# Bias matmul of the gates: contraction padded from 3 rows to 128

## The chip, the cores and the metric

The kernel runs on one core of a Trainium2 chip. The metric is the device time of one execution in microseconds (us), the median over several runs of the same program.

## The reference

There are 64 graphs of 128 nodes with 128 features. Each graph goes through an attention layer with a residual and a layer norm, and then through a relational layer with a residual and a layer norm. Cut to what the inputs leave (the adjacency holds only 0 and 1, so a single kind of edge and the `loop` relation matter), it is:

```python
# layer 0
e = leaky_relu(einsum('bid,bjd->bij', x * a_0[:, 0], x), 0.2)
alpha = softmax(where(adj == 1, e, NEG_INF))
y = layernorm(x + einsum('bij,bjd->bid', alpha, x))
# layer 1: one direction, one relation
h = y @ W_loop.T
g = h @ Wg_loop.T
vals = (h + b_loop) * sigmoid(g + bg_loop)
out = layernorm(y + relu(einsum('bnm,bmd->bnd', adj_t == 1, vals)))
```

The gates step makes `h + b_loop` and `g + bg_loop` for every node. The bias is one row of 256 numbers, the same for every node.

## The kernel before

The 64 graphs are worked in 16 groups of four. Each engine has its own written order of stages (a head, a loop body unrolled four times and run three times, a tail), and the engines meet through semaphores alone. In one pass of the body, here called a turn, TensorE does `turn_probs`, `products`, `attend`, `turn_y`, `sum_a`, `sum_b`, `gate_b`, `gate_a`, each for another group. One turn completes one stage of each kind; the body has 12 turns, and the other four groups' stages lie partly in the head and partly in the tail.

TensorE's stages, with their lines: `products` (L809, a bf16 product of a 128x128 diagonal with the `absent` tile, 512 columns, and then L813, four f32 products); `turn_probs` (L828, four transposes of the probabilities); `attend` (L838); `turn_y` (L847); `sum_a` and `sum_b` (L872); `gate_a` and `gate_b` (L858 and L861, each for two of the four graphs). An f32 product shows up in the trace as two matmul records with two weight loads.

ScalarE's turn is `weigh` (L643, makes `xat`), `exp` (L654, four), `absent` (L631), `turned_probs` (L664, copies the transposed probabilities out of PSUM), `tanh_b` and `tanh_a` (L672), `mask` (L636), `relu` (L647), `turned_y` (L668, copies the transposed y). VectorE does `values` (L762), `residual1` (L749), `scores` (L733), the statistics (L756, L781), `residual2` (L774) and `inverse` (L740). GpSimd computes the two norms (L592 to L621). SyncE issues the loads and stores.

The bias of the gates is added by a matmul of its own that opens the accumulation. `ones3` holds ones, 3 rows by 128 columns, in bf16. `b_parts` holds in three rows the three bf16 parts (high, middle, low) whose sum is the f32 bias row; it is 3 rows by 512 columns, the bias repeated for two graphs. The product adds the three parts for every node. The parts are made once by VectorE at the start (L700 to L709) and put on their rows in `place_biases` (L718 to L727), which waits on `ident`. A half of the gates step is then one bias matmul (L858) and two f32 products with `w_both` (L861, four records of 256 columns):

```python
nc.tensor.matmul(p_hg[:, half(h)], ones3[:], b_parts[:], start=True, stop=False,
                 skip_group_check=True)
for i in range(2 * h, 2 * h + 2):
    last = nc.tensor.matmul(p_hg[:, i], y_t[:, k, i], w_both[:], start=False, stop=(i % 2 == 1),
                            skip_group_check=True)
```

The bias matmul runs 32 times, twice for each group. The constants are set by GpSimd (L575 to L581) and the tile `warm` by VectorE (L697). Code for general adjacencies stands behind the loop and is skipped for these inputs.

Of the kernel before, what the change touches and what calls it, by code (L numbers as in the profile page):

```python
# [8 lines left out]
BF16 = mybir.dt.bfloat16  # L9
# [4 lines left out]
P = 128  # L14
# [56 lines left out]
def program(nc, x, x_t, adj, a_0, a_all, w, wg_t, b_loop, b_fwd, b_bwd, out):  # L71
# [9 lines left out]
    with ExitStack() as ctx:  # L81
        def sb(name, shape, dt=F32):
            return ctx.enter_context(nc.sbuf_tensor(name, shape, dt))

        def ps(name, shape, dt=F32):
            return ctx.enter_context(nc.psum_tensor(name, shape, dt))

        def sem(name):
            return ctx.enter_context(nc.semaphore(name))

        warm = sb("warm", [P, P])
        ident = sb("ident", [P, P])
        penalties = sb("penalties", [P, P], BF16)
        ones3 = sb("ones3", [3, P], BF16)
        ones_col = sb("ones_col", [P, 1])
        minus_half = sb("minus_half", [P, G])
        minus_one = sb("minus_one", [P, G])
# [9 lines left out]
        b_rest = sb("b_rest", [3, 2, 2 * P])  # L107
        b_part = sb("b_part", [3, 3, 2 * P], BF16)
        b_sum = sb("b_sum", [3, 2, 2 * P], BF16)
        b_parts = sb("b_parts", [3, 2, 2 * P], BF16)  # L110

        x_s = sb("x_s", [P, 4, G, P])
        adj_s = sb("adj_s", [P, 4, G, P], I32)
# [35 lines left out]
        p_hg = ps("p_hg", [P, G, 2, P])  # L149
# [11 lines left out]
        const_done = sem("const_done")  # L161
        ident_done = sem("ident_done")
        w_step = sem("w_step")
        b_step = sem("b_step")
        w_pe = sem("w_pe")
        w_ready = sem("w_ready")
        sum_done = sem("sum_done")
# [141 lines left out]
        def general_pool(pool):  # L309
            pool.wait_ge(general_known, 1)  # L310
            found = pool.value_load(general[0:1, 0:1], min_val=0, max_val=1)
            with pool.If(found > 0):
                with pool.Fori(0, 2 * n_graphs) as n:
                    wait_alone(nc.gpsimd, g_mv_ready, n + 1)
                    nc.gpsimd.tensor_scalar(g_var[:], g_mv[:, 1:2], EPS, None, ALU.add).then_inc(g_var_ready, 1)
                    pool.wait_ge(g_var_ready, n + 1)
                    nc.gpsimd.tensor_tensor(g_rstd[:], g_var[:], minus_half[:, 0:1], ALU.pow)\
                        .then_inc(g_rstd_ready, 1)
            pool.nop()
# [151 lines left out]
        def wait_alone(eng, semaphore, value):  # L471

            eng.wait_ge(semaphore, value)
            eng.sem_inc(wait_over[eng], 1)

        def half(h):
            return slice(h * G // 2, (h + 1) * G // 2)

        def is_first(g, n=1):

            return isinstance(g, int) and g < n

        def is_late(g):

            return isinstance(g, int) and g >= n_groups - LATE
# [87 lines left out]
        @block.gpsimd  # L573
        def _(pool):
            nc.gpsimd.memset(ident[:], 0.0).then_inc(const_done, 1)  # L575
            nc.gpsimd.memset(penalties[:], 0.0).then_inc(const_done, 1)
            nc.gpsimd.memset(ones3[:], 1.0).then_inc(const_done, 1)
            nc.gpsimd.memset(ones_col[:], 1.0).then_inc(const_done, 1)
            nc.gpsimd.memset(minus_one[:], -1.0).then_inc(const_done, 1)

            nc.gpsimd.memset(minus_half[:], -0.5).then_inc(cent_done, 1)  # L581
            pool.wait_ge(const_done, 2)
            for m, fill in ((ident, 1.0), (penalties, -PENALTY)):
                nc.gpsimd.affine_select(out=m[:], in_=m[:], compare_op=ALU.not_equal, fill=fill, base=0,
                                        pattern=[[-1, P]], channel_multiplier=1).then_inc(ident_done, 1)
            pool.wait_ge(const_done, 5)
            pool.wait_ge(cent_done, 1)

            def norm1(g, s):
                k = s % 2  # L590
                wait_alone(nc.gpsimd, st1_done, 2 * (g + 1))
                nc.gpsimd.tensor_scalar(rs1[:, k, 0], st1[:, s, :, 2], 1.0 / P, EPS, ALU.mult, ALU.add).then_inc(pool1, 1)  # L592
                pool.wait_ge(pool1, 2 * g + 1)
                nc.gpsimd.tensor_tensor(rs1[:, k, 1], rs1[:, k, 0], minus_half[:], ALU.pow).then_inc(pool1, 1)  # L594
                pool.wait_ge(pool1, 2 * g + 2)
                nc.gpsimd.tensor_tensor(y[:, s], res1[:, k], rs1[:, k, 1, :, None].broadcast_to([P, G, P]),  # L596
                                        ALU.mult).then_inc(y_done, 1)

            def norm2(g, s):
                k = s % 2  # L600
                wait_alone(nc.gpsimd, st2_done, 2 * (g + 1))
                nc.gpsimd.tensor_scalar(rs2[:, s, 0], st2[:, s, :, 2], 1.0 / P, EPS, ALU.mult, ALU.add).then_inc(pool2, 1)
                if is_late(g):
                    nc.gpsimd.tensor_tensor(shift[:, s, 0], st2[:, s, :, 1], minus_one[:], ALU.mult).then_inc(shift_done, 1)
                    pool.wait_ge(pool2, 2 * g + 1)
                    nc.gpsimd.tensor_tensor(rs2[:, s, 1], rs2[:, s, 0], minus_half[:], ALU.pow).then_inc(pool2, 1)
                    pool.wait_ge(pool2, 2 * g + 2)
                    pool.wait_ge(shift_done, 2 * (g - n_groups + LATE) + 1)
                    nc.gpsimd.tensor_tensor(shift[:, s, 1], shift[:, s, 0], rs2[:, s, 1], ALU.mult).then_inc(shift_done, 1)
                    return  # L610
                if not is_first(g):
                    pool.wait_ge(out_done, g)
                nc.gpsimd.tensor_tensor(cent[:], res2[:, k], st2[:, s, :, 1:2].broadcast_to([P, G, P]),  # L613
                                        ALU.subtract).then_inc(cent_done, 1)
                pool.wait_ge(pool2, 2 * g + 1)
                nc.gpsimd.tensor_tensor(rs2[:, s, 1], rs2[:, s, 0], minus_half[:], ALU.pow).then_inc(pool2, 1)  # L616
                pool.wait_ge(pool2, 2 * g + 2)
                pool.wait_ge(cent_done, g + 2)
                if not is_first(g, 2):
                    pool.wait_ge(stored[k], 16 * ((g - k) // 2))  # L620
                nc.gpsimd.tensor_tensor(out_s[:, k], cent[:], rs2[:, s, 1, :, None].broadcast_to([P, G, P]),  # L621
                                        ALU.mult).then_inc(out_done, 1)

            run("gpsimd", {"norm1": norm1, "norm2": norm2})
            general_pool(pool)
# [70 lines left out]
        def _(dve):  # L696
            nc.vector.memset(warm[:], 0.0).then_inc(warm_ready, 1)  # L697

            dve.wait_ge(b_loaded, 16)
            nc.vector.tensor_scalar(b_rest[:, 0, 0:P], b_rows[:, 0:P], 0.5, None, ALU.mult).then_inc(b_step, 1)  # L700
            nc.vector.tensor_copy(b_rest[:, 0, P:2 * P], b_rows[:, P:2 * P]).then_inc(b_step, 1)
# [16 lines left out]
            def place_biases():  # L718
                dve.wait_ge(ident_done, 1)
                nc.vector.tensor_scalar(b_sum[:, 0], b_part[:, 0], ident[0:3, 0:1], None, ALU.mult).then_inc(b_step, 1)  # L720
                dve.wait_ge(b_step, 7)
                nc.vector.scalar_tensor_tensor(out=b_sum[:, 1], in0=b_part[:, 1], scalar=ident[0:3, 1:2],
                                               in1=b_sum[:, 0], op0=ALU.mult, op1=ALU.add).then_inc(b_step, 1)
                dve.wait_ge(b_step, 8)
                for k in range(2):
                    nc.vector.scalar_tensor_tensor(out=b_parts[:, k], in0=b_part[:, 2], scalar=ident[0:3, 2:3],
                                                   in1=b_sum[:, 1], op0=ALU.mult, op1=ALU.add).then_inc(b_step, 1)  # L727

            def scores(g, s):
# [66 lines left out]
        def _(pe):  # L796
# [53 lines left out]
            def gate(g, s, h):  # L850
                if not is_first(g):
                    pe.wait_ge(vals_done[h], g)
                k = s % 2
                if is_first(g):
                    pe.wait_ge(w_ready, 2)
                    pe.wait_ge(b_step, 10)
                pe.wait_ge(yt_done, g + 1)
                nc.tensor.matmul(p_hg[:, half(h)], ones3[:], b_parts[:], start=True, stop=False,  # L858
                                 skip_group_check=True)
                for i in range(2 * h, 2 * h + 2):  # L860
                    last = nc.tensor.matmul(p_hg[:, i], y_t[:, k, i], w_both[:], start=False, stop=(i % 2 == 1),  # L861
                                            skip_group_check=True)
                last.then_inc(hg_done[h], 1)
# [51 lines left out]
```

## Time and profile before

| | us |
|---|---|
| median of 3 runs | 132.62 |
| lowest, highest | 131.41, 133.52 |
| the profiled execution, its own time | 132.06 |
| its span, from the first to the last instruction | 130.2 |
| PE (matmul) busy | 114.8 |
| ACT busy | 98.8 |
| DVE busy | 82.9 |
| POOL busy | 81.4 |

The span is what the profile shows; 1.86 us of the execution lie around it. PE is TensorE's matmul side and PEld its weight loads, which can run while a matmul is under way. A matmul's duration in the trace holds its way through the array, so that two neighbours overlap in the records: what a product costs is read from one start to the next, not from its duration. An idle stretch whose releaser is called "issue" is one in which the engine waited for nothing that the profile shows.

### The profile page before, as it was taken

Reading aid. Unit: us, or ns where it says so; the run is one execution under the profiler, and the core shown is the slowest. Engines: PE = TensorE matmul, PEld = TensorE weight load, DVE = VectorE, ACT = ScalarE, POOL = GpSimd, SP = SyncE. Lnnn points to the kernel's source line nnn. Section 1 sums busy time; section 2 is a strip of 40 time slices with the busy share of each in tenths; the row PEclk is TensorE's granted clock in tenths of the full one; section 3 lists DMA queues with packets and bytes.
Section 4 is the critical chain, followed back from the end, with each engine's and each line's share of the span. In section 5 each row is a group of like instructions: output and inputs, shape, how many; then the busy total and the mean of one; then the engine's idle time right before and its main releaser. Section 6 shows DMA issues by size and latency. Waiting matters only on the chain.

```text
span 130.2 us, 2906 instructions
## 1 busy us (share of the span) xinstructions
PE 114.8 (88%) x706; PEld 93.9 (72%) x713; DVE 82.9 (64%) x336; ACT 98.8 (76%) x308; POOL 81.4 (63%) x124
## 2 busy tenths in 40 slices
PE   6767778999999999999999999999999997799500
PEld 6757567678878787878787878787878784675400
DVE  0537286635868686868686868686868686756420
ACT  4437899586979797979797979797979785767622
POOL 4000035427678787978797979797979797493340
PEclk9999999999999999999999999999999999999995
DMA  2999500592082656455646465646464202020222
GB/s 54 307 292 290 146 0 0 151 282 61 0 261 61 167 160 182 143 153 172 184 138 181 141 173 149 190 134 189 133 189 133 81 0 81 5 83 0 81 81 83
DMA packets 34768, 17.28 MB, mean 133 GB/s; under 512 B 1219, under 2 KB 34758, under 8 KB 34758
## 3 DMA queue, kind: packets, MB, share of 16 engines
q1 hardware_dynamic: 34608, 17.17, 47.2%
q8 instruction: 3, 0.05, 0.2%
q14 instruction: 7, 0.06, 0.1%
q10 hardware_dynamic: 150, 0.00, 0.1%
HBM read 12.98 MB, written 4.19 MB: 132 GB/s over the span
## 4 chain that ended last, share of the span: by engine, by line
PE 79%; ACT 10%; DMA 3%; issue 3%; DVE 1%; ACTq 0%; SPq 0%; POOL 0%; POOLq 0%; DVEq 0%
PE p_hg L861 26%; PE p_e L813 12%; PE p_ag L872 11%; PE p_o L838 10%; PE p_hg L858 8%; PE p_ut L828 5%; PE p_yt L847 5%; DMA adj_s<-adj 3%; ACT prob L654 2%; ACT absent L631 2%; PE p_e L809 2%; ACT prob_t L664 2%; ACT xat L643 1%; ACT rel L647 1%; ACT out_s L683 1%
## 5 line engine op out<-in xcount | busy, mean ns | idle before, releaser
L861 PE MATMUL p_hg<-w_both,y_t 128*128 128x256 f32 x128 | 36.2, 405 | 0.0
L861 PEld LDWEIGHTS p_hg<-w_both,y_t 128*128 128x128 f32 x128 | 21.7, 189 | 8.9 <-issue 7.3
L762 DVE SCALAR_TENSOR_TENSOR vals<-th,p_hg 128x256 f32<-128x256 f32 x32 | 12.4, 418 | 20.1 <-ACT th L672 20.1
L654 ACT ACTIVATE prob<-nscore,nmax 128x128 f32<-128x128 f32 x64 | 24.7, 389 | 0.4 <-DVE nmax L733 0.4
L592 POOL TENSOR_SCALAR rs<-st 128x4 f32<-128x4 f32 x16 | 3.2, 197 | 33.6 <-DVE st L756 33.6
L749 DVE SCALAR_TENSOR_TENSOR res<-p_o,rz,x_s 128x128 f32<-128x128 f32 x64 | 18.0, 344 | 8.4 <-PE p_o L838 4.3
L838 PE MATMUL p_o<-x_s,prob_t 128*128 128x128 f32 x128 | 17.5, 280 | 2.3 <-ACT prob_t L664 2.3
L813 PE MATMUL p_e<-xt,xat 128*128 128x128 f32 x128 | 18.6, 292 | 0.7 <-ACT absent L631 0.4
L872 PE MATMUL p_ag<-vals,mask 128*128 128x128 f32 x128 | 17.9, 277 | 1.4 <-issue 1.3
L813 PEld LDWEIGHTS p_e<-xt,xat 128*128 128x128 f32 x128 | 18.4, 208 | 0.6
L838 PEld LDWEIGHTS p_o<-x_s,prob_t 128*128 128x128 f32 x128 | 15.5, 192 | 3.3 <-ACT prob_t L664 3.3
L664 ACT ACTIVATE prob_t<-p_ut 128x512 f32<-128x512 f32 x16 | 9.6, 598 | 10.8 <-PE p_ut L828 10.8
L872 PEld LDWEIGHTS p_ag<-vals,mask 128*128 128x128 f32 x128 | 16.0, 191 | 2.3 <-issue 2.0
L596 POOL TENSOR_TENSOR y<-res,rs 128x512 f32<-128x512 f32 x16 | 16.7, 1041 | 1.3
L594 POOL TENSOR_TENSOR rs<-rs,minus_half 128x4 f32<-128x4 f32 x16 | 16.2, 1013 | 1.5 <-POOL rs L592 0.3
L733 DVE CUSTOM_DVE_ANT_0 nscore<-p_e,rel 128x128 f32<-128x128 f32 x64 | 14.7, 285 | 3.1 <-ACT rel L647 2.9
L672 ACT ACTIVATE th<-p_hg 128x256 f32<-128x256 f32 x32 | 10.9, 384 | 4.2 <-PE p_hg L861 4.1
L621 POOL TENSOR_TENSOR out_s<-cent,rs 128x512 f32<-128x512 f32 x12 | 12.5, 1041 | 1.6 <-POOL rs L616 1.0
L668 ACT ACTIVATE y_t<-p_yt 128x512 f32<-128x512 f32 x16 | 9.5, 597 | 4.0 <-PE p_yt L847 4.0
L781 DVE BATCH_NORM_STATS2 st<-res 128x6 f32<-128x256 f32 x32 | 12.2, 424 | 0.6
L613 POOL TENSOR_TENSOR cent<-res,st 128x512 f32<-128x512 f32 x12 | 12.6, 1047 | 0.0
L643 ACT ACTIVATE xat<-xt,a_col 128x512 f32<-128x512 f32 x16 | 11.4, 713 | 1.4 <-DMA xt<-x_t 1.4
(63 smaller groups left out, 182.4 us busy)
## 6 DMA issues: line engine op xcount, KB each, us to landing
xt<-x_t SPq DMA_DIRECT2D x16, 256.0 KB, 3.2
adj_s<-adj SPq DMA_DIRECT2D x16, 256.0 KB, 3.9
x_s<-x SPq DMA_DIRECT2D x16, 256.0 KB, 4.1
out<-out_s SPq DMA_DIRECT2D x15, 256.0 KB, 2.3
out<-out_s SPq DMA_DIRECT2D x2, 128.0 KB, 1.8
w_rows<-w SPq DMA_DIRECT2D x1, 192.0 KB, 4.5
wg_s<-wg_t SPq DMA_DIRECT2D x1, 192.0 KB, 4.8
a_col<-a ACTq DMA_DIRECT2D x1, 0.5 KB, 3.0
```

The lines of the kernel that those rows point to most:

```text
L594: nc.gpsimd.tensor_tensor(rs1[:, k, 1], rs1[:, k, 0], minus_half[:], ALU.pow).then_inc(pool1, 1)
L596: nc.gpsimd.tensor_tensor(y[:, s], res1[:, k], rs1[:, k, 1, :, None].broadcast_to([P, G, P]), ALU.mult).then_inc(y_done, 1)
L613: nc.gpsimd.tensor_tensor(cent[:], res2[:, k], st2[:, s, :, 1:2].broadcast_to([P, G, P]), ALU.subtract).then_inc(cent_done, 1)
L621: nc.gpsimd.tensor_tensor(out_s[:, k], cent[:], rs2[:, s, 1, :, None].broadcast_to([P, G, P]), ALU.mult).then_inc(out_done, 1)
L643: nc.scalar.activation(xat[:, s % 2], xt[:, s], ACT.Copy, scale=a_col[:]).then_inc(xat_done, 1)
L654: nc.scalar.activation(prob[:, k, i], nscore[:, k, i], ACT.Exp, scale=-1.0, bias=nmax[:, s, i:i + 1], accum_out=psumz[:, s, i:i + 1]).then ...
L733: nc.vector.tensor_tensor_reduce(nscore[:, k, i], p_e[:, k, i], rel4[:, k, i], -SLOPE, FLOAT_MAX, ALU.add, ALU.min, nmax[:, s, i:i + 1]).t ...
L749: nc.vector.scalar_tensor_tensor(out=res1[:, k, i], in0=p_o[:, i], scalar=rz[:, s, i:i + 1], in1=x_s[:, s, i], op0=ALU.mult, op1=ALU.add). ...
L813: last = nc.tensor.matmul(p_e[:, k, i], xat[:, k, i], xt[:, s, i], start=False, stop=(i == G - 1), skip_group_check=True)
L838: last = nc.tensor.matmul(p_o[:, i], prob_t[:, k, i], x_s[:, s, i], start=True, stop=True)
L861: last = nc.tensor.matmul(p_hg[:, i], y_t[:, k, i], w_both[:], start=False, stop=(i % 2 == 1), skip_group_check=True)
L872: last = nc.tensor.matmul(p_ag[:, i], mask[:, s, i], vals[:, k, i], start=True, stop=True)
```

## The change

The ones become a tile of 128 rows, and `b_parts` gets 128 rows as well. VectorE sets all of `b_parts` to zero at the start, in front of its wait for the bias, and `place_biases` then writes rows 0 to 2 after a wait for that. The matmul has the same result, the same 512 columns and the same place in the order; it contracts over 128 rows, of which 125 add one times zero.

```diff
-        ones3 = sb("ones3", [3, P], BF16)
+        ones = sb("ones", [P, P], BF16)
...
-        b_parts = sb("b_parts", [3, 2, 2 * P], BF16)
+        b_parts = sb("b_parts", [P, 2, 2 * P], BF16)
...
+        b_zeroed = sem("b_zeroed")
...
-            nc.gpsimd.memset(ones3[:], 1.0).then_inc(const_done, 1)
+            nc.gpsimd.memset(ones[:], 1.0).then_inc(const_done, 1)
...
             nc.vector.memset(warm[:], 0.0).then_inc(warm_ready, 1)
 
+            nc.vector.memset(b_parts[:], 0.0).then_inc(b_zeroed, 1)
+
             dve.wait_ge(b_loaded, 16)
...
                 dve.wait_ge(b_step, 8)
+                dve.wait_ge(b_zeroed, 1)
                 for k in range(2):
-                    nc.vector.scalar_tensor_tensor(out=b_parts[:, k], in0=b_part[:, 2], scalar=ident[0:3, 2:3],
+                    nc.vector.scalar_tensor_tensor(out=b_parts[0:3, k], in0=b_part[:, 2], scalar=ident[0:3, 2:3],
                                                    in1=b_sum[:, 1], op0=ALU.mult, op1=ALU.add).then_inc(b_step, 1)
...
-                nc.tensor.matmul(p_hg[:, half(h)], ones3[:], b_parts[:], start=True, stop=False,
+                nc.tensor.matmul(p_hg[:, half(h)], ones[:], b_parts[:], start=True, stop=False,
                                  skip_group_check=True)
```

## Rows read from the trace of the kernel before

**Rows 1.** The page's chain that ended last, as shares of the span by engine

```profile
PE 79%; ACT 10%; DMA 3%; issue 3%; DVE 1%; ACTq 0%; SPq 0%; POOL 0%; POOLq 0%; DVEq 0%
```

**Rows 2.** Busy time by stretch: two turns (header first, then the stretch)

```profile
core 0: us, PE busy (x) PEld busy (x) DVE busy (x) ACT busy (x) POOL busy (x), PEclk, DMA share, GB/s
56.20:69.30 13.10, 13.05 (x86) 10.81 (x87) 9.65 (x41) 11.19 (x38) 10.85 (x14) 1.00 0.55 160
```

**Rows 3.** PE's timeline over one turn (start, us, engine, line, operation, count)

```profile
63.49 0.60 PE L828 MATMUL p_ut<-ident,prob 128*128 128x128 f32 x4
63.93 0.38 PE L809 MATMUL p_e<-absent,penalties 128*128 128x512 bf16 x1
64.15 1.05 PE L813 MATMUL p_e<-xt,xat 128*128 128x128 f32 x8
65.04 1.06 PE L838 MATMUL p_o<-x_s,prob_t 128*128 128x128 f32 x8
65.93 0.60 PE L847 MATMUL p_yt<-ident,y 128*128 128x128 f32 x4
66.37 1.06 PE L872 MATMUL p_ag<-vals,mask 128*128 128x128 f32 x8
67.36 0.38 PE L858 MATMUL p_hg<-b_parts,ones 3*128 3x512 bf16 x1
67.67 1.13 PE L861 MATMUL p_hg<-w_both,y_t 128*128 128x256 f32 x4
70.02 0.60 PE L828 MATMUL p_ut<-ident,prob 128*128 128x128 f32 x4
```

**Rows 4.** Weight loads of the same turn (PEld timeline)

```profile
63.82 0.10 PEld L809 LDWEIGHTS p_e<-absent,penalties 128*128 128x128 bf16 x1
63.93 0.52 PEld L813 LDWEIGHTS p_e<-xt,xat 128*128 128x128 f32 x3
...
67.35 0.09 PEld L858 LDWEIGHTS p_hg<-b_parts,ones 3*128 3x128 bf16 x1
67.67 0.73 PEld L861 LDWEIGHTS p_hg<-w_both,y_t 128*128 128x128 f32 x4 [0.23 <-issue]
68.73 0.09 PEld L858 LDWEIGHTS p_hg<-b_parts,ones 3*128 3x128 bf16 x1 [0.33 <-issue]
```

**Rows 5.** PE's timeline, the last two L861 records of the first half

```profile
68.21 0.59 PE L861 MATMUL p_hg<-w_both,y_t 128*128 128x256 f32 x2
```

**Rows 6.** ACT's timeline, one turn

```profile
60.05 0.60 ACT L668 ACTIVATE y_t<-p_yt 128x512 f32<-128x512 f32 x1 [0.25 <-PE p_yt L847]
...
62.69 0.62 ACT L631 ACTIVATE absent<-adj_s 128x512 bf16<-128x512 int32 x1
...
64.13 0.60 ACT L664 ACTIVATE prob_t<-p_ut 128x512 f32<-128x512 f32 x1 [0.73 <-PE p_ut L828]
...
66.57 0.60 ACT L668 ACTIVATE y_t<-p_yt 128x512 f32<-128x512 f32 x1 [0.19 <-PE p_yt L847]
```

**Rows 7.** Timelines of ACT and PE in the head: `absent` and L809 behind it

```profile
19.21 0.62 ACT L631 ACTIVATE absent<-adj_s 128x512 bf16<-128x512 int32 x1
20.06 0.38 PE L809 MATMUL p_e<-absent,penalties 128*128 128x512 bf16 x1 [0.15 <-ACT absent L631]
```

**Rows 8.** VectorE at the start, groups by line: count, busy and mean, idle before

```profile
L700 DVE TENSOR_SCALAR b_rest<-b_rows 3x128 f32<-3x128 f32 x1 | 0.2, 215 | 3.2 <-DMA b_rows<-b_loop 3.2
L697 DVE MEMSET warm<- 128x128 f32 x1 | 0.2, 165 | 0.8 <-PEq L908 0.8
```

**Rows 9.** PE's timeline: first turn of the body, and start of the tail

```profile
30.76 0.60 PE L828 MATMUL p_ut<-ident,prob 128*128 128x128 f32 x4
...
109.21 0.60 PE L828 MATMUL p_ut<-ident,prob 128*128 128x128 f32 x4
```

**Rows 10.** ACT's timeline in the tail: last tanh, waiting for the last gates

```profile
121.25 0.38 ACT L672 ACTIVATE th<-p_hg 128x256 f32<-128x256 f32 x1 [0.99 <-PE p_hg L861]
```

**Rows 11.** PE's timeline: twenty products at half clock, at the start

```profile
1.05 4.63 PE L801 MATMUL p_ag<-warm 128*128 128x128 f32 x20 [1.05 <-DVE warm L697]
```

## Prediction

> **What bounds the kernel now.** I read the page's chain first. Seventy-nine per cent of the span is TensorE's own work and ten per cent ScalarE's [rows 1], so the question is what one turn of TensorE is made of. [...] TensorE is the bound, but ScalarE with 5.6 us and GpSimd with 5.4 us of work in a turn of 6.53 us stand close behind.
>
> The timeline of PE then gives the turn. It runs from one L828 to the next, 63.49 to 70.02, that is 6.53 us, and no stage in it waits for a semaphore [rows 3]. The body's twelve turns run from 30.76 to 109.21, 78.45 us, or 6.54 each, so this turn stands for all [rows 9].
>
> **What a full matmul of this kind costs, and what the thin one costs.** The kernel has a twin of the changed matmul: L809 has 128 contraction rows, bf16 and 512 columns. It starts at 63.93, and the first record of L813 follows at 64.15, 0.22 us later. Its weights were loaded from 63.82, one product ahead, and the weights of L813 from 63.93, while L809 ran [rows 3, 4]. The bias matmul with 3 rows starts at 67.36 and L861 follows at 67.67, 0.31 us later. Its weight load starts only at 67.35, together with it, and the load for L861 starts only at 67.67, with 0.23 us of idle that nothing visible ends [rows 3, 4]. So around the thin matmul the loads don't run ahead. The change makes the form of L809 out of it, and the price follows in three gaps:
>
> - Behind L858: 0.31 us to the first L861 against 0.22 for the twin, 0.09 to 0.10 us lost.
> - In L861: its first record starts at 67.67 and its third at 68.21, two steps in 0.54 us; the last two records, together 0.59 long and 0.38 each, are 0.21 apart [rows 3, 5]. So the first step is 0.33 and not 0.21 to 0.22, since its weights had not been loaded: 0.11 us lost.
> - In front of L858: the eight records of L872 start at 66.37 and each costs 0.11 (L838: eight in 65.04 to 65.93, 0.89 us), so they are through at 67.26 where L858 starts at 67.36; at the second half the fourth record of L861 started at 68.42 (68.21 and 0.21) and its 0.21 end at 68.63, where L858 starts at 68.73 [rows 3, 4, 5]. That is 0.10 us.
>
> Together 0.30 to 0.31 us for a half. The same from the other side: L858, L861, L858, L861 now take 67.26 to 70.02, 2.76 us; with a step of 0.22 for the bias and four of 0.215 for the products it is 2 x 1.08 = 2.15. **TensorE's work in a turn falls by 0.61 us, to 5.92.** With 32 halves the most there is to win is 32 x 0.305 = 9.8 us.
>
> [...] The price used here is that of the rows.
>
> **What becomes the bound then.** TensorE would have to be fed every 5.92 us. I look for the round of waits that takes longest without the gates in it. It is this one: TensorE's `turn_y` (L847) releases ScalarE's `turned_y`, behind which stand `weigh`, four `exp` and `absent` without an idle stretch, and `absent` releases L809 of the next turn, from which TensorE goes on to L847. From rows: L847 to the copy of y_t is 65.93 to 66.57, 0.64 us [rows 3, 6]. From that copy to `absent` is 60.05 to 62.69, 2.64 us [rows 6]. From the start of `absent` to an L809 that waits for it is 19.21 to 20.06, 0.85 us, its own work, the read of its accumulator and the wait's end included [rows 7]. From L809 to L847 is 63.93 to 65.93, 2.00 us [rows 3]. Sum: 0.64 + 2.64 + 0.85 + 2.00 = **6.13 us**. Today that round has 6.53 - 6.13 = 0.40 us to spare and shows nowhere; with TensorE at 5.92 it sets the turn, and TensorE idles 0.21 us in front of L809. A turn so gains 0.40 and not 0.61 us.
>
> Of the other rounds none is longer. ScalarE's own work is 11.19 / 2 = 5.6 us plus the waits that today stand in it (0.73 in front of `prob_t`, 0.19 in front of y_t, [rows 6]); the first shrinks when the gates in front of L828 get shorter. GpSimd has 5.4 us of work and VectorE 4.8 [rows 2]. The DMA is no bound either: a share of 0.55 at 160 GB/s [rows 2] becomes 0.59 with a turn of 6.13.
>
> **The other edits.** VectorE's new memset of 128x512 bf16 lies ahead of a wait for the bias of 3.2 us. The nearest row is L697, 165 ns for 128x128 f32; four times that, as a bound from above, is 0.66 us and the bound from below 0.17 us, and both vanish in the 3.2 us [rows 8]. Without that cover the whole would cost 0.66 us once. GpSimd's memset of the ones has the same columns on more rows; I take nothing. The added wait for `b_zeroed` is met long before.
>
> **The sum, by stretches.**
>
> - Head. The four halves of groups 0 and 1 come before 30.76. The halves of group 0 end in a tanh that waits for them: the first is shorter by about 0.28 (no full gap in front), the second by 0.20 (its gap in front is counted, the one behind it isn't on the path): 0.48. Those of group 1 are followed by L828 and give 0.61. Together 1.1 us.
> - Body. L809 stands in all 12 turns. The first has the head's gain. Each of the eleven steps from one L809 to the next gains 0.40: 4.4 us. Behind the last L809, the gates of group 13 have no L809 to wait for and give TensorE's full 0.61. At 109.21 [rows 9] the gain is 1.1 + 4.4 + 0.6 = 6.1 us.
> - Tail. The last tanh waits 0.99 us for the last gates [rows 10], so these are on the path and give about 0.48 as in the head. For the gates of group 14 there are other waits nearby (the transposes of y for GpSimd's norm), so I take 0.3 of 0.61; the bounds are 0 and 0.61. Together 0.8 us.
>
> Sum 6.9 us. The profiled execution took 132.06 us (130.2 of span and 1.86 around it), so it would take 125.2. It lies 0.56 under the median; from the median the forecast is 132.62 - 6.9 = 125.7. I say **125.6 us**. Its own range: if the wait from `absent` costs 0.1 less or more in each of eleven turns, it is 124.5 to 126.8.
>
> **Rivals.**
>
> - TensorE stays the bound to the end: the round through `absent` is shorter than I read it, and each turn gains 0.61. Then 11 x 0.21 = 2.3 us more, a gain of 9.2, about 123.4 us. For it: the sum rests on an order of events read from starts. Against it: each of its four terms is a row. Chance 0.14.
> - Only part of the gaps goes. [...] With one of the three gaps gone (0.10 x 32 = 3.2 us) it is 129.4; with two, 0.2 x 32 = 6.4, it is 126.2, near the forecast. Or another round, at 6.3 us, holds the turn: 11 x 0.17 less, 127.5. Against it: the twin L809 stands between f32 products as well, and has no gap. Chance 0.17.
> - Nothing changes: the gaps come from the accumulation opened in `p_hg` or from the 256-column products, not from the 3 rows. Then the time is 132.6. For it: the table has no other 3-row matmul. Against it: L809 opens an accumulation too. Chance 0.10. [...]
> - Slower: with all 128 rows at work in the bias matmul the granted clock falls for a stretch. Products at the lower level cost 4.63 / 20 = 0.23 us a record [rows 11] against 0.11, so each us of TensorE's work costs another one. It starts to make the kernel slower than today once more than 6.9 us of the some 90 us of packed work run at that level, and 2% slower at 9.6 us. Against it: the clock is at 1.00 with the other 128-row work [rows 2], and the added rows multiply zeros. With 12 us at that level: 132.6 - 6.9 + 12 = 137.7. Chance 0.03.
>
> The forecast's own chance is 0.56. A range of 123.0 to 129.2 leaves out the no-change case, the slower one, and a little of the part case and of what lies under 123. Two per cent of the median is 2.65 us, about what a measurement of this kernel can tell from no change. Faster by more than that: 0.86; within: 0.11; slower: 0.03.
>
> **What would show it.** In the changed profile L858 should stand with 128 rows, its weight load 0.1 us or more ahead of it; L861 should follow 0.22 us behind it, without the 0.23 us of idle; a half should take 1.08 us. The turn from L828 to L828 should be 6.1 us, and in front of L809 there should be a wait for `absent` of about 0.2 us that isn't there now. The idle of ScalarE in front of `prob_t` should fall from 0.73 to some 0.1 to 0.2. If L809 shows no wait and the turn is 5.9, the first rival has it; if L861 still follows at 0.31, the gaps were not those of the three rows, and the prediction fails in its first step.

## The result, and the profile after

The changed kernel takes 125.37 us, the median of 4 runs (124.86 to 126.77), beside 133.03 us for the kernel before (131.41 to 133.52). The ratio is 0.948 with a 95% interval of 0.935 to 0.961. Run again beside its variants it gave 125.28 us against 132.38, a ratio of 0.954 (0.946 to 0.962). Here and below the ratios compare only the faster executions of each kernel, so they aren't the quotients of the medians. The forecast was 125.6 us.

The profiled execution has a span of 124.9 us. Its chain that ended last, by engine, answers to [rows 1]:

```profile
PE 63%; ACT 9%; DMA 8%; POOL 6%; DVE 4%; issue 4%; SPq 3%; ACTq 1%; POOLq 0%; DVEq 0%
```

TensorE held 79 per cent of that chain and now holds 63. The timeline of PE over one turn of the changed kernel (start, us, engine, line, operation, count) answers to [rows 3]; the bias matmul is now L862, the products behind it L865, the transposes that begin a turn L832:

```profile
62.28 0.60 PE L832 MATMUL p_ut<-ident,prob 128*128 128x128 f32 x4
62.80 0.39 PE L813 MATMUL p_e<-absent,penalties 128*128 128x512 bf16 x1
63.03 1.05 PE L817 MATMUL p_e<-xt,xat 128*128 128x128 f32 x8
63.92 1.06 PE L842 MATMUL p_o<-x_s,prob_t 128*128 128x128 f32 x8
64.81 0.60 PE L851 MATMUL p_yt<-ident,y 128*128 128x128 f32 x4
65.25 1.06 PE L876 MATMUL p_ag<-vals,mask 128*128 128x128 f32 x8
66.19 0.38 PE L862 MATMUL p_hg<-b_parts,ones 128*128 128x512 bf16 x1
66.40 1.02 PE L865 MATMUL p_hg<-w_both,y_t 128*128 128x256 f32 x4
67.27 0.38 PE L862 MATMUL p_hg<-b_parts,ones 128*128 128x512 bf16 x1
67.48 1.03 PE L865 MATMUL p_hg<-w_both,y_t 128*128 128x256 f32 x4
68.34 0.60 PE L832 MATMUL p_ut<-ident,prob 128*128 128x128 f32 x4
68.86 0.39 PE L813 MATMUL p_e<-absent,penalties 128*128 128x512 bf16 x1
```

The bias matmul at 66.19 is followed by its product at 66.40, 0.21 us later, where it was 0.31. The four records of L865 take 0.87 us to the next start, where it was 1.06. One half, 66.19 to 67.27, is 1.08 us. Before, the second started 1.37 us behind the first. The turn, 62.28 to 68.34, is 6.06 us, where it was 6.53.

The weight loads of the same stretch (PEld timeline) answer to [rows 4]:

```profile
66.16 0.10 PEld L862 LDWEIGHTS p_hg<-b_parts,ones 128*128 128x128 bf16 x1
66.19 0.83 PEld L865 LDWEIGHTS p_hg<-w_both,y_t 128*128 128x128 f32 x4
67.05 0.10 PEld L862 LDWEIGHTS p_hg<-b_parts,ones 128*128 128x128 bf16 x1
67.27 0.84 PEld L865 LDWEIGHTS p_hg<-w_both,y_t 128*128 128x128 f32 x4
```

The first load for L865 begins at 66.19, with the bias matmul, and not with the product that needs it. The second bias matmul's load begins at 67.05, 0.22 us ahead of it. The idle marked "issue" is gone. The first bias matmul's load is only 0.03 us ahead: it stands behind the wait for the copy of y_t. ScalarE's timeline of that turn answers to [rows 6]:

```profile
65.45 0.60 ACT L669 ACTIVATE y_t<-p_yt 128x512 f32<-128x512 f32 x1 [0.28 <-PE p_yt L851]
...
68.09 0.62 ACT L632 ACTIVATE absent<-adj_s 128x512 bf16<-128x512 int32 x1
68.98 0.60 ACT L665 ACTIVATE prob_t<-p_ut 128x512 f32<-128x512 f32 x1 [0.18 <-PE p_ut L832]
```

The idle in front of `prob_t` has fallen from 0.73 to 0.18 us. The next turn's L813 starts at 68.86, and `absent` at 68.09, so 0.77 us lie between the two. L832 starts at 68.34 and has four steps of 0.11 us, up to 68.78. So PE stands idle for 0.08 us in front of L813, where it had run without a gap. The forecast was 0.2.

VectorE's timeline at the start, with the memset and the first waiting instruction behind it, answers to [rows 8]:

```profile
1.00 0.27 DVE L700 MEMSET b_parts<- 128x256 uint32 x1
4.22 0.21 DVE L703 TENSOR_SCALAR b_rest<-b_rows 3x128 f32<-3x128 f32 x1 [2.95 <-DMA b_rows<-b_loop]
```

It was issued as 256 words of 4 bytes, took 0.27 us and shortened the wait behind it from 3.2 to 2.95 us; L703 starts at 4.22.

### The profile page after: what moved, and what is told of

Same layout as the page of the kernel before. It is cut to its first block, busy times and chain, and to the rows that moved or that the text cites. A ratio compares the mean times of both kernels' runs of the same rounds, so it can differ in the third digit from the quotient of the medians.

```text
span 124.9 us, 2915 instructions
## 1 busy us (share of the span) xinstructions
PE 108.8 (87%) x713; PEld 95.9 (77%) x713; DVE 82.9 (66%) x337; ACT 99.0 (79%) x308; POOL 81.3 (65%) x124
## 4 chain that ended last, share of the span: by engine, by line
PE 63%; ACT 9%; DMA 8%; POOL 6%; DVE 4%; issue 4%; SPq 3%; ACTq 1%; POOLq 0%; DVEq 0%
PE p_hg L865 17%; PE p_o L842 11%; PE p_e L817 10%; PE p_ag L876 9%; DMA adj_s<-adj 5%; PE p_hg L862 5%; PE p_ut L832 4%; PE p_yt L851 4%; PE p_e L813 3%; DMA xt<-x_t 3%; ACT prob L655 2%; ACT prob_t L665 2%; ACT absent L632 2%; ACT out_s L684 1%; DVE st L785 1%
## 5 line engine op out<-in xcount | busy, mean ns | idle before, releaser
L865 PE MATMUL p_hg<-w_both,y_t 128*128 128x256 f32 x128 | 32.8, 379 | 0.0
L865 PEld LDWEIGHTS p_hg<-w_both,y_t 128*128 128x128 f32 x128 | 24.2, 189 | 4.5
L842 PE MATMUL p_o<-x_s,prob_t 128*128 128x128 f32 x128 | 18.3, 288 | 2.3 <-ACT prob_t L665 2.3
L842 PEld LDWEIGHTS p_o<-x_s,prob_t 128*128 128x128 f32 x128 | 16.4, 200 | 3.5 <-ACT prob_t L665 3.5
L648 ACT ACTIVATE rel<-p_e 128x512 f32<-128x512 f32 x16 | 9.7, 604 | 3.9 <-PE p_e L817 3.9
```

What stands on the lines that cost most here:

```text
L842: last = nc.tensor.matmul(p_o[:, i], prob_t[:, k, i], x_s[:, s, i], start=True, stop=True)
```

## Where the time went, by stretches

The table takes the start of the first body turn's transposes, the start of the tail's, and the span's end, from the PE timelines ([rows 9] and these two rows of the changed kernel):

```profile
31.61 0.60 PE L832 MATMUL p_ut<-ident,prob 128*128 128x128 f32 x4
...
104.79 0.60 PE L832 MATMUL p_ut<-ident,prob 128*128 128x128 f32 x4
```

| | before | after | gain | forecast |
|---|---|---|---|---|
| head, to the first turn | 30.76 | 31.61 | -0.85 | 1.1 |
| body, twelve turns | 78.45 | 73.18 | 5.27 | 5.0 |
| tail, to the span's end | 21.0 | 20.1 | 0.9 | 0.8 |

Every fourth turn, where the loop starts over, is a little longer (6.15 us, and 6.58 before), and one turn of the changed kernel, from 49.76, took 6.37.

The head lost time in this pair of executions, and this isn't the change. From the first bias matmul to the first turn it is 23.72 to 30.76 before and 25.65 to 31.61 after, 7.04 and 5.96 us: the gates gain 1.08, as forecast. The loss lies ahead of them, in the first stages. There `attend` and `products` of the changed kernel, from 15.32 to 19.32, had records of 2.07 and 1.91 us where those of before have 1.16 and 1.05. One row of before and three of after:

```profile
14.98 1.16 PE L838 MATMUL p_o<-x_s,prob_t 128*128 128x128 f32 x8 [0.69 <-ACT prob_t L664]
```

```profile
15.32 2.07 PE L842 MATMUL p_o<-x_s,prob_t 128*128 128x128 f32 x8 [0.69 <-ACT prob_t L665]
...
17.61 1.91 PE L817 MATMUL p_e<-xt,xat 128*128 128x128 f32 x8
19.32 0.67 PE L832 MATMUL p_ut<-ident,prob 128*128 128x128 f32 x4
```

The busy time by stretch of the changed kernel gives the granted clock (the columns are those of [rows 2]):

```profile
11.00:13.00 2.00, 2.00 (x10) 1.95 (x10) 0.70 (x3) 1.31 (x8) 0.00 (x0) 0.50 1.17 290
...
19.00:21.00 2.00, 1.28 (x9) 1.05 (x9) 1.03 (x9) 1.44 (x3) 1.23 (x3) 0.89 0.00 0
```

The granted clock stood at 0.50 from 11 to 19 us and rose between 19 and 21 us (0.89 in that stretch, 1.00 behind it). The two stages cost 0.91 and 0.86 us more than where the clock reads 1.00 (1.16 and 1.05 us).

How long this lasts differs from one execution to the next, in both kernels. The profiled execution of the kernel before had records of that length too, up to about 13 us, though its column of the clock doesn't read 0.50. Its eight records of L813 from 10.98 are as long as those above from 17.61 (1.91 us), and yet the stretch reads 1.00 (first PE's timeline, then the stretch):

```profile
10.98 1.91 PE L813 MATMUL p_e<-xt,xat 128*128 128x128 f32 x8
```

```profile
11.00:13.00 2.00, 2.00 (x11) 2.00 (x10) 1.17 (x4) 1.13 (x7) 0.00 (x0) 1.00 1.18 290
```

So the mean granted clock that each run has is a guide to this loss and not a measure of it. It also counts the end of the span, where the changed kernel's clock reads 0.50 from 122 us on with no matmul to slow (none has a record from 121 us on). Most runs with the same mean clock took the same time, but the profiled execution of before (0.986) took 132.06 us where four others at 0.985 and 0.986 took 130.0 to 130.3, two of before at 0.973 and 0.975 took 132.4, and one run of the changed kernel at 0.948 took 124.86 where others at 0.944 to 0.947 took 126.8 to 127.2.

With that reserve, the two kernels can be compared at like clocks. The kernel before took 131.3 to 131.9 us at 0.972 and 0.973 (six runs of the first set of experiments, mean 131.5), and the changed kernel 124.8 to 125.3 at 0.971 to 0.974 (four runs of the second set, mean 125.0): 6.5 us. At 0.948 and 0.949 before took 133.3 to 133.9 (mean 133.5), and after, at 0.946, 126.8 and 126.9: 6.6 us. Within the second set alone, where before has few runs, it is about 6.8 and 7.0. The sum of the prediction was 6.9.

## The experiments

**Which number of rows removes the gaps.** Three kernels are the changed one with another number of rows, 32, 64 or 65 in place of P:

```diff
-        ones = sb("ones", [P, P], BF16)
+        ones = sb("ones", [65, P], BF16)
-        b_parts = sb("b_parts", [P, 2, 2 * P], BF16)
+        b_parts = sb("b_parts", [65, 2, 2 * P], BF16)
```

> The changed kernel with 32 rows in the ones and in b_parts instead of 128. Theory A (the gaps come with the change between a matmul on part of the array's rows and one on all of them): 32 rows are still a part, so the gaps stay: 0.31 us from the bias matmul to the first product behind it, a half of the gates 1.37, a turn 6.53, about 133 us as before the change. Theory B (the gaps come from a very small number of rows, or from the unaligned 3): 32 full rows behave like 128, step 0.22, turn 6.06, about 125.4 us.

Measured: 132.31 us (131.29 to 133.68) beside 132.30, ratio 1.005 (0.999 to 1.011). In its timeline the first product follows the bias matmul after 0.32 us, the loads of L865 stand idle for 0.23 us, and a turn has 6.52 us.

> The changed kernel with 64 rows instead of 128. [...] Theory C (the cost falls with the number of rows loaded, by a share for each missing row): half the saving, step about 0.26, turn 6.3, about 129 us.

Measured: 132.71 us (131.38 to 134.18), ratio 1.008 (1.002 to 1.014). Theory A of the kernel with 32 rows, carried to 64, gives about 133 us with a step of 0.31.

> The changed kernel with 65 rows, one more than a half of the array. Theory A in its sharp form (what counts is whether the matmul needs the whole array, not how many rows carry data): 65 rows don't fit a half, so all gaps go: step 0.22, turn 6.06, about 125.4 us, the same as 128 rows. Theory C (a share for each row): about the same as 64 rows, near 129 us. A theory by which all 128 rows must be filled: 133 us.

Measured: 126.82 us (125.64 to 127.19), ratio 0.963 (0.950 to 0.976). At the same clock of 0.946 its two runs (126.98, 127.19) stand beside 126.8 and 126.9 of the kernel with 128 rows. First the PE and then the PEld timeline of the kernel with 64 rows:

```profile
68.00 0.39 PE L862 MATMUL p_hg<-b_parts,ones 64*128 64x512 bf16 x1
68.31 1.13 PE L865 MATMUL p_hg<-w_both,y_t 128*128 128x256 f32 x4
69.38 0.39 PE L862 MATMUL p_hg<-b_parts,ones 64*128 64x512 bf16 x1
```

```profile
68.31 0.73 PEld L865 LDWEIGHTS p_hg<-w_both,y_t 128*128 128x128 f32 x4 [0.23 <-issue]
69.37 0.09 PEld L862 LDWEIGHTS p_hg<-b_parts,ones 64*128 64x128 bf16 x1 [0.33 <-issue]
```

and the same of the kernel with 65:

```profile
67.68 0.38 PE L862 MATMUL p_hg<-b_parts,ones 65*128 65x512 bf16 x1
67.90 1.03 PE L865 MATMUL p_hg<-w_both,y_t 128*128 128x256 f32 x4
68.76 0.60 PE L832 MATMUL p_ut<-ident,prob 128*128 128x128 f32 x4
```

```profile
67.47 0.10 PEld L862 LDWEIGHTS p_hg<-b_parts,ones 65*128 65x128 bf16 x1
67.68 0.84 PEld L865 LDWEIGHTS p_hg<-w_both,y_t 128*128 128x128 f32 x4
```

With 64 rows the step is 0.31 us, the loads stand idle 0.23 and 0.33 us as in [rows 4], and a turn has 6.53 us. With 65 the step is 0.22, the second bias load runs 0.21 us ahead, and a turn has 6.06. One row more does all of it. So the cost doesn't fall with each row, and the 128 need not be filled: with 3, 32 and 64 rows the step is 0.31 to 0.32 us, with 65 and 128 it is 0.21 to 0.22. That the need for the whole array decides is the author's reading; the traces show the steps and not what lies behind them. These kernels also hold the change's other edits, the memset and its wait. With 32 and 64 rows they gain nothing (ratios of 1.005 and 1.008, at most 1.014), so all of the gain comes from having more than 64 rows.

**Is it paid for each thin matmul, or for each change to and from a thin one.** In the kernel before, the 3-row matmul is cut in two:

```diff
-                nc.tensor.matmul(p_hg[:, half(h)], ones3[:], b_parts[:], start=True, stop=False,
-                                 skip_group_check=True)
+                for n in range(2):
+                    nc.tensor.matmul(p_hg[:, 2 * h + n], ones3[:], b_parts[:, n], start=(n == 0), stop=False,
+                                     skip_group_check=True)
```

> The kernel before the change, its 3-row bias matmul cut into two 3-row matmuls of 256 columns, one behind the other. Theory A (a gap for each change between part and whole, none between two of a kind): from the first thin one to the second 0.11 us, from the second to the product 0.20, a turn still 6.53 us, no change of time within 1% (133 us). Theory D (every thin matmul pays for itself, whatever stands beside it): 32 more thin matmuls at 0.1 to 0.3 us on the path, a turn of 6.7 to 7.1 us, 136 to 142 us.

Measured: 132.61 us (130.14 to 133.62) beside 132.30. PE's timeline:

```profile
67.44 0.39 PE L859 MATMUL p_hg<-b_parts,ones 3*128 3x256 bf16 x2
67.75 1.13 PE L862 MATMUL p_hg<-w_both,y_t 128*128 128x256 f32 x4
```

Both thin ones together take the same 0.31 us that one of 512 columns took, and the turn stays at 6.53. So between two of a kind there is no gap.

The converse puts the two bias matmuls of a group side by side, still with 3 rows. The half that comes first then waits for `values` of both halves:

```diff
+                first = 0 if isinstance(g, int) and (g < 2 or g >= n_groups - 2) else 1
                 if not is_first(g):
                     pe.wait_ge(vals_done[h], g)
+                    if h == first:
+                        pe.wait_ge(vals_done[1 - h], g)
...
-                nc.tensor.matmul(p_hg[:, half(h)], ones3[:], b_parts[:], start=True, stop=False,
-                                 skip_group_check=True)
+                if h == first:
+                    for n in (h, 1 - h):
+                        nc.tensor.matmul(p_hg[:, half(n)], ones3[:], b_parts[:], start=True, stop=False,
+                                         skip_group_check=True)
```

> The kernel before the change with both 3-row bias matmuls of a group issued back to back, in front of the products of the half that comes first. Theory A (0.31 us for each pair of changes between part and whole of the rows): one pair of changes in a turn instead of two, so the turn is 6.53 - 0.31 = 6.22 us and, with 0.2 for each of the four groups in head and tail, about 4.5 us less than before, near 128 us. Rival (the loss is paid for each thin matmul): turn 6.53, 132.4 us.

Measured: 128.68 us (126.81 to 129.96) beside 131.71, so 3.0 us less in the medians where 4.5 was expected. The four runs lie far apart in clock (0.937 to 0.974); the one at 0.974 took 126.81, where before took 131.6, 4.8 us less. PE's timeline:

```profile
59.12 0.60 PE L863 MATMUL p_hg<-b_parts,ones 3*128 3x512 bf16 x2
59.65 1.99 PE L866 MATMUL p_hg<-w_both,y_t 128*128 128x256 f32 x8
61.48 0.60 PE L828 MATMUL p_ut<-ident,prob 128*128 128x128 f32 x4
```

Two thin matmuls take 0.53 us, 0.21 and 0.31, and the turn is 6.22 us, as forecast from one pair of changes fewer at 0.31. So 0.31 of the 0.47 us that the padding gains in a turn is there without padding, by order alone.

**What sets the turn after the change.** The changed kernel beside three variants of it. The base for them:

> The changed kernel once more, beside its variants on one chip: the base for them. Both theories: a turn of 6.06 us and about 125.4 us. If the spread between executions comes from how long TensorE has the lower clock level in the head, time and mean granted clock go together: about 126.8 us at 0.947, 125.0 at 0.971, some 1.8 us apart.

Measured: 125.28 us (124.81 to 127.24), turns of 6.03 to 6.15 but for two of 6.17 and 6.88. Its seven runs fall in two groups: 126.8 to 127.2 us at a mean clock of 0.944 to 0.946 and 124.8 to 125.3 at 0.971 to 0.974, 1.9 us apart. Clock and time go together in this set.

The product that reads `absent` behind the four others of its stage:

```diff
-                pe.wait_ge(absent_done, g + 1)
-                nc.tensor.matmul(p_e[:, k], penalties[:], absent[:, k], start=True, stop=False, skip_group_check=True)
...
-                    last = nc.tensor.matmul(p_e[:, k, i], xat[:, k, i], xt[:, s, i], start=False, stop=(i == G - 1),
-                                            skip_group_check=True)
-                last.then_inc(e_done, 1)
+                    nc.tensor.matmul(p_e[:, k, i], xat[:, k, i], xt[:, s, i], start=(i == 0), stop=False,
+                                     skip_group_check=True)
+                pe.wait_ge(absent_done, g + 1)
+                nc.tensor.matmul(p_e[:, k], penalties[:], absent[:, k], start=False, stop=True, skip_group_check=True)\
+                    .then_inc(e_done, 1)
```

> The changed kernel with the bf16 product that reads `absent` moved behind the four f32 products of its stage, so that it is wanted 0.89 us later. Theory R (the turn of 6.06 us is set by the round turn_y, y_t, exp, absent, first product): the wait for absent goes and the turn falls to what TensorE needs, 5.92 plus the 0.05 that the bias matmul waits for y_t, so 5.97; eleven turns by 0.09 make 1.0 us, a ratio to the changed kernel of 0.992. Rival (another round of the same length, or ScalarE's own work, holds the turn): 6.06 stays, ratio 1.00.

Measured: 122.54 us (121.75 to 125.06), ratio to before 0.933 (0.924 to 0.941), so 2.7 us below the changed kernel where 1.0 was expected. PE's timeline:

```profile
60.29 0.60 PE L832 MATMUL p_ut<-ident,prob 128*128 128x128 f32 x4
60.72 1.06 PE L815 MATMUL p_e<-xt,xat 128*128 128x128 f32 x8
61.83 1.05 PE L842 MATMUL p_o<-x_s,prob_t 128*128 128x128 f32 x8
...
66.25 0.60 PE L832 MATMUL p_ut<-ident,prob 128*128 128x128 f32 x4
```

The body does what the theory says: the products follow the transposes after 0.43 us, and a turn is 5.96 to 5.98, apart from 6.03 where the loop starts over and a long one of 6.57. The surplus is in the head, which the expectation left out: the first turn begins at 29.77, where the changed kernel beside it begins at 31.26. Only a part of this is the wait for `absent`. The second group's products, in the changed kernel beside it and then in this one:

```profile
10.15 0.61 PE L813 MATMUL p_e<-absent,penalties 128*128 128x512 bf16 x1 [2.69 <-ACT absent L632]
10.55 1.91 PE L817 MATMUL p_e<-xt,xat 128*128 128x128 f32 x8
```

```profile
9.66 1.13 PE L815 MATMUL p_e<-xt,xat 128*128 128x128 f32 x8 [2.76 <-ACT xat L644]
```

They start 0.49 us earlier without the wait. The larger part is the clock: the eight f32 records take 0.96 us to the next start here and 1.70 there, since the granted clock from 9 to 11 us is 1.00 here and 0.56 there. Whether the earlier start is what kept the clock up isn't shown.

`absent` made for the first four groups only:

> The changed kernel in which ScalarE makes the absent tile for the first four groups only and the later products read what stands there: left out are twelve of sixteen absent activations, and the output's masking is that of other groups. Theory R: as for the moved product, a turn of about 5.97 us, TensorE bound, 124.4 us; ScalarE's 0.7 us of freed time brings nothing beyond that. Rival (ScalarE's total work sets the turn): a turn shorter by up to 0.7 us on ScalarE and so TensorE at its floor of 5.92 too, but then the moved product would have stayed at 6.06; the pair decides.

The kernel also sets `sums`, which the omitted activations would write, to zero at the start.

Measured: 124.19 us (122.17 to 125.66), turns of 5.97 but for two of 6.04 and 6.03 and two long ones of 6.27 and 6.43. With 0.7 us less work on ScalarE in each turn the turn is that of the moved product. So it is the wait and not ScalarE's load that held 6.06. What is left, 5.97, is TensorE's own 5.92 and 0.05 in front of the first bias matmul. In four profiles (this kernel, the changed one, the one with the moved product and the one without the bias matmul) the gates start 0.14 us behind the end of the copy of y_t (in the rows of the changed kernel, 66.05 to 66.19), while the products in front of them are through 0.05 us before. No run takes this wait away.

No bias matmul at all (the gates then open with L865):

> The changed kernel without the bias matmul; left out is the bias of both gates. Theory R (the gates lie outside the round that sets the turn): the turn stays 6.06 us, TensorE only idles longer in front of the absent product, about 0.6 us; only the eight halves in head and tail give 0.2 each where they are on the path, 1.0 to 1.6 us in all, about 124 us. Rival (TensorE is still what bounds the turn): each turn falls by 0.43 to 5.63, twelve turns and the ends make 6.7 us, about 118.7 us.

Measured: 124.81 us (123.58 to 125.38), turns of 6.05 and 6.06, but for a long one of 6.44 and those where the loop starts over. PE's timeline, with L863 for the products of the gates:

```profile
71.48 1.97 PE L863 MATMUL p_hg<-w_both,y_t 128*128 128x256 f32 x8
73.28 0.60 PE L832 MATMUL p_ut<-ident,prob 128*128 128x128 f32 x4
74.15 0.39 PE L813 MATMUL p_e<-absent,penalties 128*128 128x512 bf16 x1 [0.27 <-ACT absent L632]
```

The gates take 1.80 us in place of 2.15, and all of it is handed to the wait in front of L813. The twelve turns take 73.18 us, as in the first profile of the changed kernel, so there the bias matmul costs nothing in the body. What is left of it is in head and tail: 0.5 us in the medians, 0.8 and 0.3 us in the two profiles of this set, and 1.3 us between the runs at like clocks (123.58 at 0.975, 124.8 and 124.9 at 0.974 and 0.973). In the body TensorE isn't the bound any more.

**Was the moved product a gain already before the change.** The same edit on the kernel before:

> The kernel before the change (3-row bias matmul) with the product that reads `absent` moved behind the four f32 products, as in late_penalty. Theory R (before the change TensorE's own work sets the turn and the round through absent has 0.4 us to spare): the body's turn stays 6.53 us; only the head, where TensorE waits for absent, gains the 1.5 us it gained in late_penalty, about 130.9 us. Rival (the order of the products helps TensorE itself): turns of 6.4 us or less, about 129 us.

Measured: 130.65 us (129.96 to 131.99), ratio 0.994 (0.990 to 0.998). The turn stays at 6.52 to 6.59, and at clocks of 0.972 and 0.973 its runs take 130.7 to 131.5 where before takes 131.2 to 131.7, 0.5 us less in the mean. Before the change TensorE didn't wait for `absent` in the body, and moving the product brings only the head's share, which was less than the 1.5 us expected. In the medians the move was worth 2.7 us after the change and about 1 before.

**The long turns.** The kernels above with turns of 6.22 us or less have one or two long ones that begin between 48 and 57 us. From the timelines of the changed kernel's second profile, first SyncE's row of the load concerned and then ScalarE's:

```profile
49.69 0.37 SPq L531 DMA_DIRECT2D xt<-x_t  x1
```

```profile
53.88 0.72 ACT L644 ACTIVATE xat<-xt,a_col 128x512 f32<-128x512 f32 x1 [0.62 <-DMA xt<-x_t]
```

The load of `xt` was issued at 49.69, behind a store's wait, and `xat` started 4.2 us later, after 0.62 us of waiting. In this profile the median from issue to landing of these loads is 3.5 us, so this one was slow to land as well. The experiment issues the loads one store earlier:

```diff
             reload(0, 0)
+            reload(1, 1)
...
-                for s in range(1, UNROLL + 1):
+                for s in range(2, UNROLL + 2):
                     g = turn * UNROLL + s
                     reload(g, s % UNROLL)
-                    store(g - 1, (s - 1) % UNROLL)
+                    store(g - 2, (s - 2) % UNROLL)
```

> The changed kernel with SyncE issuing each group's loads ahead of one more store than now (the store of group g-2 instead of g-1 stands between two sets of loads). Theory L (the one or two long turns, the fourth and fifth of the body at 6.17 to 6.88 us, come from a load of xt that SyncE issues behind a store and that lands 0.6 us late): all turns 6.03 to 6.15, about 0.6 us less than the changed kernel. Rival (the long turns come from traffic in the DMA queues or from something else): they stay, or others grow, since the stores come later.

Measured: 124.81 us (123.74 to 125.45), ratio to before 0.949 (0.940 to 0.957). The twelve turns are 6.03 to 6.16 with no long one, 72.87 us in all against 73.69 in the profile of the changed kernel before it. With both edits together, below, there is no long turn either. So the long turns come from loads of `xt` that arrive too late, and issuing them earlier is enough. How much of the lateness is the store in front and how much the slow landing isn't shown. The gain of 0.5 us in the medians lies within their spread.

> Both at once: the absent product last in its stage and the loads ahead of one more store, on the changed kernel. Theories R and L: turns of 5.97 to 6.03 us throughout, about 0.6 us below late_penalty, 122 us. If theory L falls: 122.5 us as late_penalty.

Measured: 121.58 us (121.28 to 123.01), ratio to before 0.929 (0.922 to 0.937), turns of 5.97 to 6.04 throughout. This kernel, the padding with both edits, is the fastest of all: 10.1 us below the kernel before beside it (131.71) and some 3.7 below the changed kernel, measured in another set. At a mean clock of 0.975 it took 121.4 us, where the changed kernel took 124.9 at 0.973.

## Why the prediction was right

**The three gaps.** They were read from starts, with L809 as the twin, and were right in place and size: 0.31 to 0.21 behind the bias matmul, the loads running ahead, 1.37 to 1.08 for a half. The one exception is the gap in front of the first half, of which only 0.05 of 0.10 us went, and its load is 0.03 us ahead where 0.1 was forecast. The runs with 64 and 65 rows (steps of 0.31 and 0.22 us) and with two thin matmuls side by side (0.21 us from the first to the second, 0.31 behind the second), which the prediction did not have, tie the gaps to the change between thin and full matmuls. What makes them isn't shown. Besides the gaps of 0.10 us on either side, 0.11 us is lost since the load of the next weights doesn't run ahead across the change. The records themselves show none of this: the matmul lasts 0.38 us at 32 and at 128 rows and its load 0.09 and 0.10 us, while the step to the next product is 0.32 and 0.21 us. By the records alone the kernel would not have become faster.

**The round that takes over.** It was named rightly: L851, y_t, `exp`, `absent`, L813. It was predicted at 6.13 us and measured at 6.06. The term that was mis-sized is the one from `absent` to the product that waits for it, 0.85 us from an instance in the head [rows 7], 0.77 in the body. The other terms are as read: 0.64, 2.64 and 2.01. Eleven turns by 0.07 make 0.8 us too little gain. The first rival (TensorE stays the bound) is refuted by the kernel without the bias matmul.

**What was left out.** TensorE's own turn is 5.97 and not 5.92, since the first bias matmul starts 0.05 us late behind the copy of y_t. With this and the shorter round the idle in front of L813 is 0.08 us and not 0.21. The sentence that the DMA is no bound was wrong for one or two of twelve turns: a load that had 0.4 us a turn more to land in now costs 0.3 to 0.9 us in an execution. In the first profile this took back 0.3 of the 0.8 us that the shorter round had given, in the second all of it.

**The head and the tail.** The gates gave 1.08 us in the head and the tail 0.9, for 1.1 and 0.8. The clock rival did not come about: in the body (31 to 109 us) the granted clock reads 1.00, and the doubled records in the head occur in both kernels. Its price of 0.23 us a record comes from [rows 11], in a stretch whose clock column reads 1.00 in both kernels and not half; where the column does read 0.50, from 17.61 to 19.32 in the changed kernel, a record costs 0.21 us. The profile pair shows only 5.3 us of gain, because its two executions differ in how long the doubled records lasted (up to 12.69 us before, 19.32 after).

**How much of the nearness is luck.** The mechanism is shown, but that 125.4 lies 0.2 us from 125.6 is in part luck. The round read too long and the long turns left out work against each other, and executions of one kernel lie about 2 us apart, which goes with the clock. The medians give a gain of 7.7 us in the first set and 7.1 in the second, like clocks 6.5 to 7.0, for a sum of 6.9.

**The edits priced at nothing.** The memset took 0.27 us inside a wait of 3.2, between the bounds of 0.17 and 0.66, and the first instruction behind the wait starts at 4.22 us with it and without it.

## What to carry to other kernels

A small matmul between full ones can cost more than its columns (here 0.31 us where a full one has 0.22): read the step from one start to the next and compare it with a full matmul of the same columns in the same trace. If the step is longer, try more rows (here 32 and 64 changed nothing, and 65 did as well as 128), or put several such matmuls side by side (here that took 0.31 us from a turn). When a bound engine is relieved by 0.6 us, first look for the round of waits with the least slack, since here it took back 0.14 us in each turn, and moving one product then gained more than it had been worth before.

## What the runs showed of the hardware

Between 128-row f32 matmuls, a bf16 matmul of 512 columns with its product makes a half of the gates of 1.37 to 1.38 us with 3, 32 and 64 rows, and of 1.08 us with 65 and 128. The columns of a 3-row matmul were split in two with no further cost (0.31 us to the product, a turn of 6.53 us, as unsplit). Of two 3-row matmuls side by side only the second has the longer step (0.21 and 0.31 us).

The record of a matmul outlasts the step behind it by about 0.17 us: 0.38 against 0.21 for 512 bf16 columns and for 256 f32 columns, 0.28 against 0.11 for 128 f32 columns. That this is the matmul's way through the array is the author's reading. The records show only that the excess is the same for these three.

In the first 20 us the records of TensorE have twice their step (0.21 us in place of 0.11 for 128 f32 columns) for a while that differs between executions of one kernel. In the changed kernel the granted clock reads 0.50 from 11 to 19 us. The runs of before at a mean clock of 0.985 took 130.3 us and those at 0.948 took 133.5, 3.2 us apart, which is half as much as the gain of the change. The mean clock is only a guide to it: the profile of before reads 1.00 over eight records that took 1.91 us in place of 1.05. Why this lasts longer in some executions than in others stays open.
